# New cost estimates in the planner that orders a one-core attention and feed-forward kernel

## The reference

```python
def _layernorm(x, axis=-1, eps=1e-05):
    m = jnp.mean(x, axis=axis, keepdims=True)
    v = jnp.var(x, axis=axis, keepdims=True)
    return (x - m) / jnp.sqrt(v + eps)

def attention(x, w_qkv, w_proj, b_proj):
    B, S, dim = x.shape
    heads = 16
    head_dim = dim // heads
    scale = head_dim ** (-0.5)
    qkv = (x @ w_qkv).reshape(B, S, 3, heads, head_dim)
    Q, K, V = (qkv[:, :, 0], qkv[:, :, 1], qkv[:, :, 2])
    Q = apply_rope(Q)            # x * cos + concat(-x2, x1) * sin
    K = apply_rope(K)
    attn = jnp.einsum('bqhd,bkhd->bhqk', Q, K) * scale
    causal = jnp.tril(jnp.ones((S, S), dtype=bool))[None, None]
    attn = jnp.where(causal, attn, -1000000.0)
    attn = jax.nn.softmax(attn, axis=-1)
    out = jnp.einsum('bhqk,bkhd->bqhd', attn, V).reshape(B, S, dim)
    return out @ w_proj + b_proj

def ffn(x, theta, phi, theta_noise, phi_noise):
    real = jnp.einsum('bti,io->bto', x, jnp.cos(theta + theta_noise))
    imag = jnp.einsum('bti,io->bto', x, jnp.sin(phi + phi_noise))
    return jnp.sqrt(real * real + imag * imag)

x = x + attention(_layernorm(x), ...)      # x is (4, 2048, 256), float32
x = x + ffn(_layernorm(x), ...)
```

## Time and profile before

| | before |
|---|---|
| time, median of 3 runs | 2007.47 us (2006.9 to 2008.37) |
| profiled execution | 2007.47 us, its span 2005.7 us (1.8 us lie outside the span) |
| PE busy | 1965.7 us, 98% of the span |
| DVE busy | 1568.6 us, 78% |
| ACT busy | 1394.1 us, 70% |
| POOL busy | 862.3 us, 43% |
| mean granted TensorE clock | 0.995 |

### The profile page before, as it was taken

One profiled execution on the slowest core, in us unless ns is written; L12 is line 12 of the kernel. 1 busy time (PEld: TensorE's weight loads), 2 busy tenths in 40 slices (PEclk: granted clock), 3 DMA queues, 4 the chain that ended last, 5 costly groups with the idle time before them and its releaser, 6 DMA issues.

```text
span 2005.7 us, 38214 instructions
## 1 busy us (share of the span) xinstructions
PE 1965.7 (98%) x12044; PEld 785.8 (39%) x12044; DVE 1568.6 (78%) x4101; ACT 1394.1 (70%) x2687; POOL 862.3 (43%) x1336
## 2 busy tenths in 40 slices
PE   7999999999999999999999999999999999999998
PEld 4333333333443444334443343434434343433335
DVE  5988888988878788897877878798687868687925
ACT  3357767786677676887767776687766767676773
POOL 3632426353443534544363443546434363451232
PEclk9899999999999999999999999999999999999999
DMA  6310212131111221221222211222111222130131
GB/s 138 78 44 19 68 59 68 58 89 61 55 60 54 74 72 59 75 81 64 67 64 68 65 62 50 85 74 88 58 56 60 70 71 81 33 116 6 49 107 52
DMA packets 130762, 133.30 MB, mean 66 GB/s; under 512 B 29434, under 2 KB 105722, under 8 KB 130554
## 3 DMA queue, kind: packets, MB, share of 16 engines
q1 hardware_dynamic: 127728, 128.29, 20.8%
q10 hardware_dynamic: 2832, 2.56, 0.7%
HBM read 38.49 MB, written 25.68 MB: 32 GB/s over the span
## 4 chain that ended last, share of the span: by engine, by line
PE 87%; ACT 5%; POOL 2%; issue 2%; DVE 2%; DMA 1%; SPq 1%; DVEq 0%; POOLq 0%; ACTq 0%
PE banks L1074 23%; PE banks L1059 23%; PE banks L1037 22%; PE banks L981 6%; PE banks L992 5%; ACT probs L1178 3%; PE banks L1019 3%; PE banks L926 3%; DVE chunk_max L1379 1%; PE banks L908 1%; PE banks L915 1%; PE banks L1045 0%; SPq L723 0%; PE banks L1004 0%; SPq L739 0%
## 5 line engine op out<-in xcount | busy, mean ns | idle before, releaser
L1178 ACT ACTIVATE probs<-banks 128x512 f32<-128x512 f32 (+1 forms) x2240 | 1144.1, 602 | 334.5 <-PE banks L1059 303.1
L1379 DVE TENSOR_REDUCE chunk_max<-banks 128x1 f32<-128x512 f32 x1536 | 987.7, 684 | 217.5 <-PE banks L1037 214.7
L1037 PE MATMUL banks<-stack_k,stack_q 96*128 96x512 bf16 (+3 forms) x2560 | 691.2, 350 | 10.2 <-DVE chunk_max L1379 7.4
L1059 PE MATMUL banks<-stack_q,stack_k 99*128 99x512 bf16 (+3 forms) x2560 | 695.9, 350 | 4.9 <-ACT probs L1178 1.7
L1374 DVE CUSTOM_DVE_ANT_0 banks<-banks,row_mask 128x128 f32<-128x128 f32 (+3 forms) x1024 | 484.1, 508 | 113.6 <-PE banks L1037 112.8
L1074 PE MATMUL banks<-probs,v_one 128*17 128x512 f32 (+3 forms) x5120 | 543.8, 533 | 4.2 <-POOL probs L1506 2.6
L1059 PEld LDWEIGHTS banks<-stack_q,stack_k 99*128 99x128 bf16 x2560 | 230.7, 97 | 447.2 <-ACT probs L1178 237.6
L1037 PEld LDWEIGHTS banks<-stack_k,stack_q 96*128 96x128 bf16 x2560 | 233.6, 97 | 337.8 <-DVE chunk_max L1379 91.9
L1506 POOL TENSOR_SCALAR_AFFINE_SELECT probs<-probs 128x512 f32<-128x512 f32 x256 | 162.5, 644 | 304.0 <-ACT probs L1178 303.0
L1074 PEld LDWEIGHTS banks<-probs,v_one 128*17 128x17 f32 x5120 | 110.0, 96 | 263.9 <-issue 131.4
L646 POOL TENSOR_TENSOR turned<-raw,cos_t 128x512 f32<-128x512 f32 x62 | 78.8, 1271 | 225.2 <-ACT raw L1138 218.6
(11 more groups left out here) (158 smaller groups left out, 1163.4 us busy)
## 6 DMA issues: line engine op xcount, KB each, us to landing
stack_q<-parts SPq DMA_DIRECT2D x384, 64.0 KB, 2.6
stack_k<-parts SPq DMA_DIRECT2D x354, 64.0 KB, 2.6
sums<-o_raw SPq DMA_DIRECT2D x64, 256.0 KB, 2.3
rot<-raw SPq DMA_DIRECT2D x236, 64.0 KB, 2.0
xin<-x SPq DMA_DIRECT2D x16, 512.0 KB, 3.7
heads_t<-sums SPq DMA_DIRECT2D x26, 256.0 KB
mid<-x SPq DMA_DIRECT2D x13, 512.0 KB, 3.9
inverse<-inverses SPq DMA_DIRECT2D x26, 256.0 KB
```

What stands on the lines that cost most here:

```text
L1037: mm = nc.tensor.matmul(bank[:, n * wide:(n + 1) * wide], stack_q[u % 2][0:SPLIT_ROWS, t, h + n, j * P:(j + 1) * P], stack_k[u % 2][0:SPLI ...
L1059: mm = nc.tensor.matmul(bank[:, a * wide:(a + 1) * wide], stack_k[u % 2][0:ROWS, j // SUB, first + a, (j % SUB) * P:(j % SUB + 1) * P], st ...
L1178: nc.scalar.activation(probs[:, g % PROBS, first:first + many, w0:SPAN], bank, ACT.Exp).then_inc(s_exp, 1)
L1379: nc.vector.tensor_reduce(to, bank[:, 0:count * wide].rearrange("p (h n) -> p h n", h=count), AX.X, ALU.max).then_inc(s_emptied["DVE"], 1)
```

## The change

Only numbers in `plan()` change: the planned costs of fourteen kinds of jobs, in us. No instruction of the jobs is added, removed or altered, and no dependency is. `xload` goes from 0.6 to 0.45, `dev` and `dev3` from 3.2 to 2.8, `rot` 2.6 to 2.4, `fetch` 7.8 to 5.4, the DVE read of a masked `max` loses 0.04 per part, `split` 1.5 to 1.3, `rows` 2.0 to 1.7, `heads` 1.5 to 1.1, `x3` 0.65 to 0.45, `bias` 2.5 to 1.3, `keepinv` 0.65 to 0.35, `inverse` 1.4 to 1.1, `store` 0.65 to 0.35. The diff, cut to most of them:

```diff
-                job(("rot", u, c), "SP", 2.6, at, [("out", ("qk", u, c, 1)), used], 1.8)
+                job(("rot", u, c), "SP", 2.4, at, [("out", ("qk", u, c, 1)), used], 1.8)
...
-                job(("fetch", u, c), "SP", 7.8, at, [("rope", u, c, ROPE_OPS - 1), ("scores", LAST_STEP.get(u - 2), 0)], 2.2)
+                job(("fetch", u, c), "SP", 5.4, at, [("rope", u, c, ROPE_OPS - 1), ("scores", LAST_STEP.get(u - 2), 0)], 2.2)
...
-                with_bank(name, name, "DVE", (0.17 if d == tile // SUB and masks(n) else 0.07 / n) * n + wide / 970, at + step * done / total)
+                with_bank(name, name, "DVE", (0.13 if d == tile // SUB and masks(n) else 0.07 / n) * n + wide / 970, at + step * done / total)
...
-            job(("split", u, c), "POOL", 1.5, at - 0.2, [("rowmax", u, c)], TURN_LAG if u else None)
+            job(("split", u, c), "POOL", 1.3, at - 0.2, [("rowmax", u, c)], TURN_LAG if u else None)
...
-            job(("rows", u, c), "SP", 2.0, at, [("out", ("turn", u, c))], 1.8)
+            job(("rows", u, c), "SP", 1.7, at, [("out", ("turn", u, c))], 1.8)
...
-            job(("heads", n), "SP", 1.5, at, [stored, ("wave", prev, SUB - 1), ("sin", KT - 1), ("heads", n - 1), *free], 2.5)
+            job(("heads", n), "SP", 1.1, at, [stored, ("wave", prev, SUB - 1), ("sin", KT - 1), ("heads", n - 1), *free], 2.5)
...
-            job(("bias", n), "POOL", 2.5, at, [("x3", n), ("bias", n - 1)])
+            job(("bias", n), "POOL", 1.3, at, [("x3", n), ("bias", n - 1)])
...
-            job(("keepinv", n), "SP", 0.65, at, [("invert", n), ("keepinv", n - 1)], 2.2)
+            job(("keepinv", n), "SP", 0.35, at, [("invert", n), ("keepinv", n - 1)], 2.2)
...
-            job(("inverse", n), "SP", 1.4, at, [("keepinv", n), ("add", prev), ("inverse", n - 1), *free], 6.8)
+            job(("inverse", n), "SP", 1.1, at, [("keepinv", n), ("add", prev), ("inverse", n - 1), *free], 6.8)
...
-                job(("dev3", n), "POOL", 3.2, at + 0.1, [("stats3", n), ("apply3", n - 1)])
+                job(("dev3", n), "POOL", 2.8, at + 0.1, [("stats3", n), ("apply3", n - 1)])
...
-            job(("store", u, t), "SP", 0.65, at, [("lift", u, t)], 2.4)
+            job(("store", u, t), "SP", 0.35, at, [("lift", u, t)], 2.4)
...
```

6 lines of the change are left out of this document (3 added, 3 removed).

## The result

The changed kernel is slower: 2023.78 us, median of seven runs from 2015.96 to 2026.09, against 2006.96 of the kernel before (seven runs, 2006.54 to 2009.83). The ratio of the means is 1.0072 with a 95% interval of 1.0055 to 1.0088 (that of the two medians would be 1.0084). The forecast of 2005.0 was wrong, in size and in sign, and the measured time lies outside its range.

What follows compares the result with a forecast made beforehand. PE's stream was taken to bound the kernel; terms -1.5 - 1.6 - 1.9 + 0 + 1.5 + 1.05 + 0 = -2.45 on the profiled 2007.47 us gave 2005.0 us, range 1998.5 to 2013.0.

Steps and rivals of the forecast that it cites:

- What bounds the kernel: Whole kernel: PE's stream sets the end (87% of the wait chain), so only its idle time and needless work count.
- E: Unit 15 and block 11: new wait for den(11), old stall gone, fetch slack gone; +1.5 us, bounds -1 and +6.
- The rival of a lower clock: Tail: PE work at the low clock level for 5 us adds 2.5 us, giving 2007.5; chance 0.03.
- G: Steady interleave: a fifth of PE's jobs move a few places, waits for DVE halve or grow; 0, plus or minus 4.
- A: Step 80: mask(80) goes ahead of L660 on POOL, cutting PE's wait of 2.40 us; -1.5 us.
- B: PE, whole kernel: 14 fewer changes between values and other work, 0.11 us each; -1.6 us.
- C: Tail: dev3(13) ahead of the last four masks, 14 of 18 idle matmuls gone, lead earlier; -1.9 us.
- D: Head: qk(0,2) about a microsecond earlier, two idle matmuls go, but DVE is full; 0, within 0.5.
- F: Other blocks: invert(n) 3 to 4 us earlier for seven blocks, some loads and masks late; +1.05 us.
- The price argument: SP and POOL queues: jobs planned too short put those behind them ahead of others ready first; no size given.
- a rival of 0.22: Unit 15: SP and POOL queues jam at den(11) and fetch(15,3); +6.9 us, about 2014.4; chance 0.22.
- the signs of being right: Step-80 wait under 1 us, lead 1.9 sooner, block-11 idle DVE 3 to 5, PE 1 to 3, last fetch 1785 to 1793.

Runs made afterwards that it cites:

- experiment 5: changed kernel with all of block 11 (SP's sixteen jobs, invert(11), scale(11), bias(11)) put back where it stood before the change: 2015.90 us, ratio 1.0035.
- experiment 6: kernel before with block 11 alone put where the changed kernel has it: 2019.71 us, ratio 1.0056.
- experiment 1: changed kernel with invert(11) alone moved back on DVE to its place before the change: 2025.74 us, ratio 1.0093.
- experiments 2 and 7: changed kernel with modulus(2), modulus(6) moved later on ACT: 2024.12 us; changed kernel with apply, modulus and dev put back as before the change: 2033.64 us.
- experiment 13: changed kernel with prices set to the rows: fetch 7.6, bias 2.4, dev and dev3 2.95: 2011.42 us, ratio 1.0017.
- experiment 14: kernel before with the new DVE price of the masked maximum read alone, plus mask(81) directly behind mask(80) on POOL: 2004.25 us, ratio 0.9976.
- experiment 9: kernel before with one new price alone, the masked maximum read on DVE (0.13 instead of 0.17 per part): 2003.01 us, ratio 0.9976.

## Why the prediction was wrong

**What bounds the kernel**: right. In all kernels the loss that could be placed is where PE stands idle, or runs at the low clock.

**E, block 11, is the step that failed, by its size, and the term in it is the landing of `den(11)`.** Place, direction and chain were right: DVE waits for `den(11)`, PE behind it, then the last fetch. The sum took the landing at the median of 2.2 us, when its own rows had one of 6.3; it was 4.7. With 4.7 put in, its own working gives DVE 6.8 us late instead of 4.3, and 6.74 was measured. Half of that for slack was not far off, as PE waited 3.99; but 2.2 had been written down. The fetch cost 1.65 and not 0.6. And no term had the clock, 4.0 us of work at half speed, worth 2.0. So +1.5 should have been 3.99 + 1.65 - 1.34 + 2.0 = +6.3; the distance count has +5.0, experiment 5 some 7 to 8, and experiment 6, in the old lists, 12.1. Even with +6.3 for E the sum comes to 2009.8 only, so E alone does not explain 2023.8.

**The rival of a lower clock had the right mechanism in the wrong place.** It looked at the idle matmuls of the tail and was given 0.03. The clock fell at stalls in the middle: at block 11, at 1327, and in experiments 1, 2, 6 and 7 during or just behind the waits that they made longer. The Trainium skill (TensorE: Matmul & The Clock Gate, Part 1) says that the default state is throttled and that activity releases it; the traces agree, as the granted clock went from the full level to half 1.1 us into the wait of 3.99 us (0.71 over 1770 to 1780), came back after 4.0 us of work, and stayed at 1.00 when experiment 5 took the wait away.

**G, the steady interleave, taken as 0 within 4, hid a second place, and it is the other half of the miss.** The collision of `apply` and `modulus` on ACT was never looked for, since ACT's list had only 108 jobs out of place; the places in units 6 and 10 cost 2.8 and 5.3 us (the latter with a dip). With block 11 put back (experiment 5) the kernel is still 7.6 us slower, and the loss lies there. Where it lies is shown; that the collision is its cause is not, as experiments 2 and 7 moved ACT's jobs and made it worse.

**A** was handed on: 0.80 + 1.73 in place of 2.40, where -1.5 was forecast. The prediction named this as its worst case, though at `mask(82)` and `mask(83)`; it came at `mask(81)`. The slow POOL stretch came again in the changed kernel, 2.25 and 2.14 us for L652 and L654, beside the same DVE work (L1413). The rule of the Trainium skill (GPSIMD Engine Reference, Key points) that GpSimd is disturbed by DVE instructions with two SBUF inputs was right in that.

**B** can't be told from the rest (14 x 0.11 is 1.5, not 1.6). **C**: from the last `values` to `lead` 6.2 to 6.5 us were forecast and 6.2 measured; with a wait of 1.91 for the later masks the tail gained about 1.3 instead of 1.9. **D**: the two idle matmuls less changed nothing that runs agree on. **F** is near 0 for PE. DVE did stand for another `den`, in block 12, where the prediction looked for it: 5.64 us ahead of 1931.58. But PE has no wait between 1895 and 1945.

**The price argument** ("it is SP and POOL that are now planned too short") was right and was not followed. The one price changed alone towards the rows gains 0.24%, about half of it clock; the one changed alone away from them, `fetch`, loses 0.27%; the groups of SP and POOL, which hold prices moved either way, lose 1.0 and 0.65%. But these losses do not add up to the changed kernel's, and experiment 13, with three prices set to the means of the rows, is still 0.17% slower than the kernel before. So part of what a new list gains or loses is the luck of its places, and one or two lists for each group of prices can't separate the two. The argument should still have been worth more than a rival of 0.22.

**The signs.** Of the signs of being right, the wait at step 80 held (0.80), and two at block 11 were passed on the bad side: 6.74 us for DVE against 3 to 5, 3.99 for PE against 1 to 3. The last fetch went out at 1803.73 to 1811.28 instead of 1785 to 1793, of which some 12 us are what the kernel had lost by then. None of the signs of being wrong appeared (L1037 waits 9.3 us, not 11; no stall over 3 us for a fetch), though the time was 19 us above the forecast: they looked at single waits and not at the clock or at places outside the sum.

## What to carry to other kernels

Read a change of planned costs by its errors against the trace. Here the loss that could be explained came at the most crowded place. Give the worst queue the landing time that its own rows show, not the median, and price its stall with the low clock behind it. When a job is moved in one queue, move all that wait for it in the others, or the stall grows, as in experiment 1. A wait removed at one place of a busy queue was handed to the next job of that queue twice here, from `mask(80)` to `mask(81)` and from there to a split; look for that before counting a gain.

## What was not expected of the hardware

The clock fell 1 to 3 us into the long waits of PE and came back only some us after work had begun again: 6.8 us at the lower level around the wait of 3.99, 10.2 around 7.95, 13.7 around 8.93. Of these 4.0, 4.8 and 7.0 us were work, so such a wait cost about 1.3 to 1.5 times its length. Shorter waits had a dip in some executions and none in others: one behind 2.40 us at step 80 of the kernel before and behind 1.84 in experiment 14, none behind 2.54 in experiment 6 or 1.75 in experiment 9. The crowded places of units 6 and 10, with waits of 0.57, 0.30 and 0.46 us close together, had one in unit 10 alone in the changed kernel, in unit 6 alone in experiment 13, and in both in experiment 1. That is the likely reason why one kernel's times differ by 10 us from run to run, but only mean clocks are on record for the other runs. The seven of the kernel before beside it stayed within 3.3 us, other batches of it within 5.1 to 6.5.

The same small DMA of 32 KB (`den(11)`) was taken up 4.7 us after its issue in the changed kernel, 6.3 in the kernel before, 5.1 in experiment 6 and 6.8 in experiment 5, and never near the median of 2.2.
